# Softmax denominators in a fused attention and mixture-of-experts kernel: reciprocals sent through DRAM and read back eightfold, instead of being spread by a matmul

## The reference

```python
x = x + _L0_xattn_ref(_layernorm(x), ctx_1024, ctx_1024, ...)   # x: 8 x 256 x 128
x = x + _L0_ffn_ref(_layernorm(x), ...)
# in _L0_xattn_ref, H = 16 heads of Dh = 8:
A = jnp.einsum('bhqd,bhkd->bhqk', q, k) / np.sqrt(Dh)
A = jnp.where(causal, A, -jnp.inf)
w = jax.nn.softmax(A, axis=-1)
out = jnp.einsum('bhqk,bhkd->bhqd', w, v)
return out @ Wo.T + bo
# in _L0_ffn_ref:
probs = jax.nn.softmax(xt @ router_w.T); top 4 -> gate
act = gelu(up_r) * gate;  routed = act @ routed_down;  shared = gelu(up_s) @ shared_down
```

## Time and profile before

| | |
|---|---|
| median of 3 runs | 226.51 us (225.4 to 226.7) |
| profiled execution | 225.0 us |
| its span, first to last instruction | 223.0 us |
| PE busy | 188.8 us (85%) |
| DVE busy | 169.8 us (76%) |
| ACT busy | 143.2 us (64%) |
| POOL busy | 96.2 us (43%) |
| mean granted TensorE clock | 0.985 of full speed |

### The profile page before, as it was taken

The page is one execution under the profiler, slowest core; times in us unless marked ns, Lnnn a source line. Parts: engine busy times, 40 slices in busy tenths (PEclk is TensorE's granted clock), DMA queues, the critical chain, the costliest instruction groups (busy, mean ns, idle before and its releaser), DMA issues.

```text
span 223.0 us, 4896 instructions
## 1 busy us (share of the span) xinstructions
PE 188.8 (85%) x1610; PEld 138.3 (62%) x1610; DVE 169.8 (76%) x456; ACT 143.2 (64%) x276; POOL 96.2 (43%) x178
## 2 busy tenths in 40 slices
PE   0629788869999978978999999886969989999992
PEld 0316565557777746756676776455848858787871
DVE  4599978619689859959989996227968688787781
ACT  2261365726586885875777768875867976777661
POOL 5789029906457577577566565732202000000000
PEclk9999999958999999999999999999999999999999
DMA  4523333830332311312312210100000010010011
GB/s 128 155 70 99 82 95 84 259 101 19 97 84 55 105 44 50 103 47 50 99 54 75 78 31 3 31 6 24 3 1 0 3 50 0 0 47 0 0 48 47
DMA packets 23735, 12.97 MB, mean 58 GB/s; under 512 B 4696, under 2 KB 23400, under 8 KB 23712
## 3 DMA queue, kind: packets, MB, share of 16 engines
q1 hardware_dynamic: 23040, 12.52, 20.4%
q10 hardware_dynamic: 576, 0.13, 0.3%
q0 software_dynamic: 96, 0.03, 0.1%
HBM read 3.86 MB, written 1.05 MB: 22 GB/s over the span
## 4 chain that ended last, share of the span: by engine, by line
PE 49%; DVE 16%; SPq 9%; issue 8%; ACT 7%; POOL 5%; DMA 5%; POOLq 0%; DVEq 0%; ACTq 0%
SPq L328 6%; DVE sb_mx L765 5%; PE psum L955 5%; PE psum L937 3%; PE psum L874 3%; PE psum L871 3%; PE psum L914 3%; PE psum L872 3%; PE psum L856 3%; PE psum L858 3%; PE psum L857 3%; DMA sb_ctx<-in_ctx_t 2%; PE psum L863 2%; PE psum L921 2%; PE psum L918 2%
## 5 line engine op out<-in xcount | busy, mean ns | idle before, releaser
L765 DVE TENSOR_REDUCE sb_mx<-psum 128x2 f32<-128x512 f32 (+1 forms) x96 | 62.8, 678 | 10.3 <-PE psum L921 8.1
L577 ACT ACTIVATE sb_probs<-psum 128x512 f32<-128x512 f32 x96 | 55.8, 602 | 20.7 <-PE psum L937 19.0
L422 POOL TENSOR_SCALAR_AFFINE_SELECT sb_probs<-sb_probs 128x256 f32<-128x256 f32 (+1 forms) x96 | 45.2, 487 | 36.5 <-ACT sb_probs L577 35.8
L656 DVE TENSOR_TENSOR sb_probs<-sb_probs,psum 128x512 f32<-128x512 f32 x32 | 21.9, 683 | 10.1 <-ACT sb_probs L521 9.8
L521 ACT ACTIVATE sb_probs<-psum 128x512 f32<-128x512 f32 x36 | 21.5, 600 | 12.0 <-PE psum L858 11.9
L914 PE MATMUL psum<-sb_qk_op 96*128 96x256 bf16 x128 | 26.0, 286 | 0.0
L937 PE MATMUL psum<-sb_qk_op 128*128 128x256 bf16 x128 | 24.8, 276 | 0.9 <-ACT sb_probs L577 0.7
L663 DVE TENSOR_TENSOR sb_hid_l<-sb_probs,sb_hid_h 128x512 fp32r<-128x512 f32 x36 | 24.7, 685 | 0.3
L527 ACT CAST sb_hid_h<-sb_probs 128x512 fp32r<-128x512 f32 x36 | 22.2, 616 | 2.9 <-DVE sb_probs L656 2.9
L911 PE MATMUL psum<-sb_fut,sb_id_b 128*128 128x256 bf16 x64 | 18.4, 287 | 5.3 <-issue 4.4
L955 PE MATMUL psum<-sb_probs,sb_v_op 128*32 128x256 f32 x256 | 20.5, 391 | 0.8 <-ACT sb_o_raw L552 0.8
(11 more groups left out here) (114 smaller groups left out, 390.0 us busy)
## 6 DMA issues: line engine op xcount, KB each, us to landing
sb_qk_op<-sb_qk SPq DMA_DIRECT2D x96, 64.0 KB
sb_ctx<-in_ctx_t SPq DMA_DIRECT2D x8, 128.0 KB, 2.4
sb_num<-sb_o_raw SPq DMA_DIRECT2D x8, 128.0 KB, 2.1
out<-sb_o_raw SPq DMA_DIRECT2D x4, 256.0 KB, 2.3
sb_x<-in_x SPq DMA_DIRECT2D x3, 256.0 KB, 4.2
sb_up_f<-in_rup_t SPq DMA_DIRECT2D x1, 512.0 KB, 3.6
sb_dn_f<-in_rdown SPq DMA_DIRECT2D x1, 512.0 KB, 4.4
sb_x<-in_x SPq DMA_DIRECT2D x2, 128.0 KB, 3.4
```

The source lines that it names most:

```text
L422: nc.gpsimd.affine_select(out=v, in_=v, compare_op=ALU.is_ge, fill=0.0, base=0, pattern=[[0, v.shape[1]], [1, P]], channel_multiplier=-1). ...
L577: nc.scalar.activation(probs[g][:, u * BANK:(u + 1) * BANK], psum[:, BANK_S + n % SB, :], ACT.Exp, scale=float(DH) ** -0.5).then_inc(s_exp, 1)
L656: nc.vector.tensor_tensor(hid[buf[k]], gel[buf[k]], psum[:, 3 + k % 2, :], ALU.mult)\
L765: nc.vector.tensor_reduce(dst, src, AX, ALU.max).then_inc(m_max, 1)
```

## The change

The constant hrow, its load, the rden_h tile with its clearing, the float32 matmul L1029 and its use of PSUM bank 7 are gone. SP writes the reciprocals to a DRAM tensor, 16 rows of 256 for each batch. ACT waits for this write in tick 5 and then issues four DMAs, one in each of the ticks 5 to 8, each of which reads 4 heads' rows eight times into 32 rows of rden_rows. DVE waits in tick 9 for all four, and multiplies from rden_rows in SBUF instead of from PSUM.

```diff
                 c = turn.batch(3)
                 if c is not None:
                     sp.wait_ge(den_inv, count(c + 1))
-                    sp.wait_ge(rden_ps, count(c))
-                    sp.dma_start(rden_h[0:H, :], rden[:, :]).then_inc(rden_in, 16)
+                    rows = rden_d[c, :, :].rearrange("h (n s) -> (h n) s", s=H * S // P)
+                    sp.dma_start(rows, rden[:, :]).then_inc(rden_out, 16)
...
-            nc.gpsimd.memset(hrow[:, :], 0.0)
-            nc.gpsimd.memset(rden_h[:, :], 0.0)
...
+                    c = turn.batch(3)
+                    if 5 <= t < 5 + J and c is not None:
+                        j = t - 5
+                        if j == 0:
+                            act.wait_ge(rden_out, 16 * (c + 1))
+                            act.wait_ge(att_done, c)
+                        act.dma_start(rden_rows[VW * j:VW * j + VW, :], rden_d[c, G * j:G * j + G, :].partition_broadcast(DH))\
+                            .then_inc(rden_in, 16)
...
-                        dve.wait_ge(rden_in, count(16 * c))
+                        dve.wait_ge(rden_out, 16 * c)
                         nc.vector.reciprocal(rden[:, :], den[:, :]).then_inc(den_inv, 1)
                     if t == 9 and c is not None:
-                        dve.wait_ge(rden_ps, count(c + 1))
+                        dve.wait_ge(rden_in, 16 * J * (c + 1))
                         dve.wait_ge(num_in, count(16 * (c + 1)))
                         dve.wait_ge(o_ps, count(c))
-                        nc.vector.tensor_tensor(att[:, :], psum[:, BANK_B, 0:S], num[:, :], ALU.mult).then_inc(att_done, 1)
+                        nc.vector.tensor_tensor(att[:, :], rden_rows[:, :], num[:, :], ALU.mult).then_inc(att_done, 1)
...
-                    if t == 9 and c is not None:
-
-                        pe.wait_ge(rden_in, count(16 * (c + 1)))
-                        wait_bank(turn, BANK_B, "rden")
-                        mm(psum[:, BANK_B, 0:S], hrow[:, :], rden_h[:, :], start=True, stop=True).then_inc(rden_ps, 1)
```

More of the change, by code:

```diff
@@ L101, in xattn_moe_kernel @@
         spr = sb("spr", [P, (NCH - 1) * P], F32R)
-        hrow = sb("hrow", [P, P], F32)
         exno = sb("exno", [P, NR], F32)
@@ L148, in xattn_moe_kernel @@
         rden = sb("rden", [P, H * S // P], F32)
-        rden_h = sb("rden_h", [P, S], F32)
+        rden_rows = sb("rden_rows", [P, S], F32)
+        rden_d = nc.dram_tensor("rden_by_head", (NB, H, S), F32, kind="Internal").ap()
         att = sb("att", [P, S], F32)
@@ L207, in xattn_moe_kernel @@
         pv_ps, pv_read = sem("pv_ps"), sem("pv_read")
-        num_in, den_in, rden_in = sem("num_in"), sem("den_in"), sem("rden_in")
-        den_inv, rden_ps, att_done, o_ps, x2_done = sem("den_inv"), sem("rden_ps"), sem("att_done"), sem("o_ps"), sem("x2_done")
+        num_in, den_in, rden_out, rden_in = sem("num_in"), sem("den_in"), sem("rden_out"), sem("rden_in")
+        den_inv, att_done, o_ps, x2_done = sem("den_inv"), sem("att_done"), sem("o_ps"), sem("x2_done")
         stats2, rstd2, xn2_done = sem("stats2"), sem("rstd2"), sem("xn2_done")
@@ L282, in xattn_moe_kernel @@
             BANK_A: [("qk", 0, qk_less, 2, 2), ("router", 4, r_step, RSTEPS, 5), ("v", 1, v_read, 1, 1), ("gates", 4, gt_read, 1, 2)],
-            BANK_B: [("max1", 2, mt_read, 2, 2), ("xn2", 4, xh_done, 1, 1), ("max0", 1, mt_read, 2, 1), ("rden", 3, att_done, 1, 1),
+            BANK_B: [("max1", 2, mt_read, 2, 2), ("xn2", 4, xh_done, 1, 1), ("max0", 1, mt_read, 2, 1),
                      ("o", 3, x2_done, 1, 1)],
@@ L361, in turn_of @@
                     for dst, src in ((wv_sb, wv_t), (bv_sb, bv), (wo_sb, wo_t),
-                                     (rw_sb, router_t), (hrow[0:H, :], head_rows), (exno, expert_no.partition_broadcast(P)),
+                                     (rw_sb, router_t), (exno, expert_no.partition_broadcast(P)),
                                      (bo_sb, bo.partition_broadcast(P))):
@@ L778, in turn_of @@
                     if (turn.at, t) == (1, 8):
-                        dve.wait_ge(c_in, 16 * 7)
+                        dve.wait_ge(c_in, 16 * 6)
                         nc.vector.tensor_copy(bv_all[:, :], bv_sb[:, :].to_broadcast([P, P])).then_inc(bv_spread, 1)
@@ L1018, in turn_of @@
                         if c == 0:
-                            pe.wait_ge(c_in, 16 * 7)
+                            pe.wait_ge(c_in, 16 * 6)
                         for a in range(QB):
```

## The result

The changed kernel takes 240.6 us (median of 4 runs, 238.9 to 240.9), the kernel before on the same chip 226.0 us: a ratio of 1.067 [1.061, 1.073], slower by about 15 us. The forecast was 235.3 us, in a range to 241.0, and counted from 226.5 us for the kernel before; on that base the ratio gives 241.7 us, just beyond the range. The direction was right, the size too small: 14.7 us where 8.8 were forecast. The profiled execution has a span of 238.4 us, 15.4 more than before, at a mean clock of 0.950 of full speed where before has 0.985.

What follows compares the result with a forecast made beforehand. No engine was taken as a bound by itself; what counts is who waits for whom. Removed load -0.5, turns 3 to 8 +3.9, turn 10 +2.4, clock +3.0: +8.8 on 226.5 gives 235.3 us, range 230.0 to 241.0.

Steps and rivals of the forecast that it cites:

- The place: Turns 3 to 8: exp 6 waits behind the store, PE late at unit 8, 6.5 us together.
- Turn 10: GELU behind ACT's wait and two issues starts 2.4 us late, and nothing takes the delay up: +2.4 us.
- The removals: hrow's load gone, -0.5 us; float32 spreading matmul gone in turns 3 to 8, at most 2.6 us.
- The issues of reads 2 to 4: ACT's later issues lie under queued exps: nothing; upper bound 1.35 us in each turn.
- DVE's wait for the reads: DVE waits 0.5 us for the rows, beside PE's longer delay: nothing added; 0.9 us with slower reads.
- turn 9: ACT reaches the wait after the store lands: nothing, at most 0.5 us.
- Rival A: ACT blocked by its own issues in turns 3 to 8 and 10: +17.0, 243.5 us, chance 0.07.
- Rival B: ACT's and SP's issues lock each other out: +4.2 on 8.8, 239.5 us, chance 0.10.
- Rivals C and D: C: the wait doesn't bind, 223.4 us, chance 0.05; D: stalls hide but in turn 10, 227.5 us, chance 0.10.
- I take 2.1 us: SP's small store of the reciprocals to DRAM lands 2.1 us after its issue, bounds 1.9 and 3.0.
- The clock ... +3.0 us: PE's idle in turn 10 grows to 4.6 us and the clock falls once more: +3.0 us, or nothing.
- 0.45 us: ACT's issue of the first read, behind the store and ahead of exp 6, takes 0.45 us.

Runs made afterwards that it cites:

- the runs with nothing late: Kernel before without the spreading matmul and hrow's load and clearing, 221.6 us; changed kernel with four reads of the input and no wait for the store, 223.0 us.
- The run with fillers: Changed kernel plus bf16 matmuls whose result nobody reads, on PE where it waits in turns 3 to 10: 233.6 us at a clock of 0.998.

## Why the prediction fell short

**Right.** The place: ACT's wait at tick 5 makes exp 6 late and PE waits at unit 8 in the six turns 3 to 8. Turn 10: the forecast had the GELU 2.4 us late; from turn 9's projection to turn 10's it is 16.20 us against 13.94 before, 2.3 more. The removals, 3.1 us against 3.2, but with an interval of 1.2 us either way, and its part of 0.5 us for hrow's load isn't seen when that load is moved alone; the sum says little of its terms. The issues of reads 2 to 4 hidden (the run with reads alone), DVE's wait for the reads small (0.9 us at most, forecast 0.5), turn 9 at nothing (11.5, 11.6 and 11.6 us late in turns 7 to 9). Rival A fell with the run of the issues alone. Rival B too: in the changed kernel ACT's issues took 0.658 us at the least and 0.659 in the median, the 20 that overlapped an issue of SP in time like the 12 that didn't, so neither waits for the other; the rule of the Trainium skill, Perfetto Trace Analysis, section "DMA Instruction — HWDGE (DVE, Sync)", that one lock serves the sequencers, doesn't show here as a time. Rivals C and D are refuted by the result; C would have been the 221.6 to 223.0 us of the runs with nothing late.

**The step that failed first: "I take 2.1 us" for the store, one number for all turns.** The bounds were 1.9 and 3.0, from transfers within SBUF. It was 1.4 us, or 3.4 and 3.3 in turns 4 and 7, where a transfer of instructions got in its way; the mean over the six turns is (4 x 1.4 + 3.4 + 3.3) / 6 = 2.05, so the mean was right by luck, and useless. PE's stalls came out at 2.70 and 2.62 us there and at 0.7 in turns 5, 6 and 8, where the forecast had 1.1 to 1.24 in each of the five. Those two turns hold 10.4 us of the price. The 3.0 us of the earlier trace rows was the sign: it is the landing in turn 4 of the kernel before, where q8 runs as well, and I took it for a bound on all turns where it was a fact about one. No run has both stores at 1.4 us in their old place, so what they cost alone is read from the turns and not measured.

**The step that failed second: "The clock ... +3.0 us", one fall in turn 10.** It was mis-sized, and for the most part by the first: 7.0 us measured (6.1 by the ratios, and some 1.5 of it the kernel's own), by the run in which PE is kept busy. I asked which stall would be longer than the 2.71 us of the earlier trace rows, and had each of the six at unit 8 at about 1 us, because the store had one duration. The falls came in turn 3, after the stalls of 2.70 and 2.62 us in turns 4 and 7, and after PE's idle of 2.07 and 3.96 us before the projections of turns 9 and 10. With PE kept busy, the time from the projection before to those of turns 4 and 7 is 2.7 and 2.6 us shorter. A fall in turn after turn was not among the rivals at all. Nor does a row give the fall for certain. In the changed kernel PE idled 2.76 us before 45.94, as before, and both windows from 44 to 52 us have 1.00:

```profile
44.00:48.00 4.00, 2.06 (x17) 1.71 (x18) 0.46 (x1) 0.90 (x3) 0.01 (x1) 1.00 0.42 111
48.00:52.00 4.00, 3.53 (x43) 2.34 (x40) 3.93 (x9) 2.11 (x4) 3.07 (x5) 1.00 0.16 43
```

And the same idle before turn 9's projection, 2.07 us, brought a fall in the changed kernel (first line and window) and none in the run with reads and no wait (second):

```profile
163.56 0.38 PE L1035 MATMUL psum<-sb_wo,sb_att 128*128 128x128 f32 x1 [2.07 <-DVE sb_att L802]
164.00:168.00 4.00, 4.00 (x15) 3.30 (x14) 2.82 (x10) 1.75 (x4) 0.94 (x2) 0.57 0.12 37
...
147.84 0.38 PE L1035 MATMUL psum<-sb_wo,sb_att 128*128 128x128 f32 x1 [2.07 <-DVE sb_att L802]
148.00:152.00 4.00, 3.46 (x18) 2.62 (x19) 2.81 (x10) 1.98 (x4) 1.14 (x3) 1.00 0.13 37
```

**Third, the first read's issue: "0.45 us".** It was 0.66 us, 1.25 in turn 3. The issues at the start move plain tiles and these a broadcast of 32 rows, but what sets the length wasn't tried; the first read is long in the run with four reads alone too, 1.28 us with no issue of SP beside it. Unit 8 came 3.39, 4.80, 2.78, 2.78, 4.71 and 2.78 us after the store's issue in turns 3 to 8, 8.7 us later than before in all, where the forecast had 6.5.

**The sum.** Forecast: 8.9 of stalls (6.5 and 2.4), less 3.1 for the removals, and 3.0 of clock. Measured: some 12, less 3.2, and 7.0, by medians from different chips. The store to DRAM is not slow by itself. Against the 1.9 us of a transfer within SBUF its 1.4 us speaks against the Trainium skill's "surprisingly long delay" for HBM targets (Perfetto Trace Analysis, the same section), and the Trainium skill's page DMA: Bandwidth & Descriptors, section "Latency and other measured facts", which calls HBM the slowest target, isn't borne out for these 16 KB.

## What to carry to other kernels

A wait put into the stream of an engine that feeds the matmul engine is priced by its worst turns, not by its mean: find every landing of the nearest transfer in the trace, ask why the longest is long, and count a fall of the clock for each stall near the length that has brought one. When a wait and the issues behind it are in one stream, the issues are free only as long as something is queued ahead of them; behind a wait that binds, the first one lies in the open. Before blaming the new route, move the producer: one or two ticks earlier in DVE's stream in turns 3 to 7, and four in turn 10, removed 15 us that neither placement of the reads did.

## What the runs showed of the hardware

A transfer of instructions is one packet that keeps one DMA engine for 0.9 to 1.5 us, and a small transfer that is under way lands some 1.1 us after that packet's end (26 of 26): 2.9 to 3.5 us to DRAM against 1.4, 2.2 to 3.6 within SBUF against 1.9. A packet that began 1.0 us before the issue, or 1.8 us after it, did nothing (1.4 us; 1.9 within SBUF). The smaller packets of q14 near turn 3's store left it at 1.4 us in most runs (1.5, 1.7 and 2.2 in three). Landings of 2.1 us in turn 8 and 1.6 in turn 10 of the run with reads and no wait had no such packet of q8 beside them; one had ended 0.4 us before the issue of the first.

The instructions that q8 brings look like PE's. From its first packet to its last, PE has 252 to 259 recorded instructions for each packet in sixteen of the traces, and no other engine comes near that number (DVE 36 to 39). The run with fillers, which gives PE more instructions, has 13 packets where all others have 12, and moving PE's code moved the packets of four turns. Why it left the two beside turns 4 and 7 in place is open.

A store of 16 KB to DRAM took 0.33 us of SP's sequencer and landed in 1.4 us; the transfer of the same bytes within SBUF took 0.61 and 1.9. The first goes out as 128 rows of 128 bytes and the second into 16 rows; what sets the difference was not tried.

The granted clock is not the same in all executions of one kernel: with the wait alone, four runs had 0.991, 0.969, 0.955 and 0.955, and 230.7, 232.7, 235.6 and 236.7 us.
